# Second attention's queries projected four batches at a time, its first keys loaded earlier, and weights quantised during the first attention

## What is computed

```python
x = x + attention(layernorm(x), ctx, ctx, Wq, bq, Wk, bk, Wv, bv, Wo, bo)   # 16 heads of 16
x = x + experts(layernorm(x), classifier, bias, gate_up, down)              # router, top 6 of 40, 32 of them real experts
x = x + attention(layernorm(x), ctx, ctx, ...)                              # softmax of -0.25 * q.k
x = x + fp4_ffn(layernorm(x), w_gate, w_up, w_down)

def fp4_quant_dequant(x):            # in blocks of 16, for the weights and the activations
    scale = max(max(abs(block)) / 6, 1e-12)
    return GRID[searchsorted(MID, abs(block / scale))] * sign(block) * scale
```

## Time and profile before

| | |
|---|---|
| time, median of 3 runs (lowest, highest) | 1060.65 us (1060.6, 1065.75) |
| the profiled execution's own time | 1065.29 us |
| its span, first to last instruction | 1063.7 us |
| busy: PE, DVE, ACT, POOL | 932.7, 697.2, 414.1, 136.6 us |
| DVE row maxima (L1219), 256 | 235.5 us |
| quantising the weights on DVE, 16 batches x 9 instructions | 1.89 us more DVE time in a batch than in the first attention |
| front of the second attention, from 613.98 to the first row scores at 657.66 | PE busy 23.3 of 43.7 us, granted TensorE clock 0.79 |
| from there to the first column scores at 672.79 | PE busy 10.5 of 15.1 us, granted clock 0.73 |
| both attentions, steady part | granted clock 1.00 |

### The profile page before, as it was taken

One profiled execution on the slowest core, in us unless ns is written; L12 is line 12 of the kernel. 1 busy time (PEld: TensorE's weight loads), 2 busy tenths in 40 slices (PEclk: granted clock), 3 DMA queues, 4 the chain that ended last, 5 costly groups with the idle time before them and its releaser, 6 DMA issues.

```text
span 1063.7 us, 20769 instructions
## 1 busy us (share of the span) xinstructions
PE 932.7 (88%) x7430; PEld 724.7 (68%) x7430; DVE 697.2 (66%) x1518; ACT 414.1 (39%) x970; POOL 136.6 (13%) x129
## 2 busy tenths in 40 slices
PE   2996999999979779999998856899999987898987
PEld 1663778788857459899988745577777765455554
DVE  4454677777735715455554464788888874999995
ACT  1441566666655441111111122466565654111211
POOL 7021000000011430000000004000000001344442
PEclk9997999999986999999999978899999988999999
DMA  9688454454042630202121305554444200000000
GB/s 284 198 235 192 85 101 91 95 88 88 17 132 62 200 130 16 78 16 62 35 61 60 109 26 129 112 91 88 88 87 88 60 2 1 5 12 10 13 13 18
DMA packets 103231, 87.07 MB, mean 82 GB/s; under 512 B 44002, under 2 KB 94562, under 8 KB 103010
## 3 DMA queue, kind: packets, MB, share of 16 engines
q1 hardware_dynamic: 103122, 85.58, 33.3%
HBM read 67.52 MB, written 17.79 MB: 80 GB/s over the span
## 4 chain that ended last, share of the span: by engine, by line
issue 32%; PE 28%; DVE 27%; DMA 7%; SPq 2%; POOL 2%; ACT 1%; POOLq 0%; DVEq 0%; ACTq 0%
PE ps L794 12%; DVE ext L1219 8%; PE ps L801 7%; DMA qscr<-qsp 3%; DVE Pr L1167 2%; DVE Pr L1172 2%; DVE Pr L1170 2%; DMA Qz<-mT 2%; PE ps L651 2%; PE ps L561 2%; DMA wgu<-wgu 1%; DVE amh L1399 1%; DVE Pr L1421 1%; POOL ksp L492 1%; PE ps L700 1%
## 5 line engine op out<-in xcount | busy, mean ns | idle before, releaser
L1219 DVE TENSOR_REDUCE ext<-ps 112x2 f32<-112x750 f32 x256 | 235.5, 933 | 56.8 <-PE ps L623 54.3
L986 ACT ACTIVATE Pr<-ps 125x448 f32<-125x448 f32 x384 | 199.0, 542 | 101.9 <-PE ps L637 88.7
L794 PE MATMUL ps<-xT,wgu 128*128 128x224 f32 x704 | 150.1, 356 | 12.5 <-issue 4.9
L794 PEld LDWEIGHTS ps<-xT,wgu 128*128 128x128 f32 x704 | 132.9, 191 | 23.1 <-issue 12.4
L637 PE MATMUL ps<-Qz,Kp 98*125 98x224 f16 x768 | 132.8, 269 | 15.8 <-DMA Qz<-mT 13.7
L623 PE MATMUL ps<-Kp,Qz 96*112 96x375 f16 x512 | 123.8, 334 | 11.8 <-DMA Qz<-qscr 10.6
L637 PEld LDWEIGHTS ps<-Qz,Kp 98*125 98x125 f16 x768 | 96.4, 140 | 49.9 <-DMA Qz<-mT 18.6
L691 PE MATMUL ps<-wv,ctx 128*125 128x256 f32 x384 | 121.9, 402 | 0.8 <-ACT Vx L992 0.7
L561 PE MATMUL ps<-ctx,wk 128*128 128x375 f32 x256 | 95.1, 519 | 25.0 <-DMA bqk<-bqk 14.2
L1337 DVE TENSOR_TENSOR Pr<-Pr,ps 128x224 f32<-128x224 f32 x88 | 34.1, 388 | 125.5 <-ACT Pr L1057 68.2
L873 PE MATMUL ps<-Pr 128*112 128x352 f32 x256 | 85.5, 480 | 16.9 <-DVE Pr L1421 16.5
(11 more groups left out here) (139 smaller groups left out, 1094.9 us busy)
## 6 DMA issues: line engine op xcount, KB each, us to landing
ctx<-ctxT SPq DMA_DIRECT2D x64, 375.0 KB, 3.7
Kp<-kscr SPq DMA_DIRECT2D x96, 187.5 KB, 4.1
kscr<-ksp SPq DMA_DIRECT2D x32, 375.0 KB, 3.8
wgu<-wgu SPq DMA_DIRECT2D x32, 256.0 KB, 2.8
Qz<-qscr SPq DMA_DIRECT2D x192, 28.0 KB, 3.9
wdn<-wdn SPq DMA_DIRECT2D x32, 128.0 KB, 3.0
qscr<-qsp SPq DMA_DIRECT2D x32, 112.0 KB, 3.3
X<-x_in SPq DMA_DIRECT2D x1, 1792.0 KB, 11.7
```

The source lines that it names most:

```text
L794: last = mm(ps[:, bank, half_ * CT:(half_ + 1) * CT], wgu_sb[e % NE][:, q, EI * half_:EI * half_ + EI], xT2[:, q, c * CT:(c + 1) * CT], st ...
L986: A(Pr[g % 2][0:KC, j, GI * t:GI * t + GI, :].rearrange("r h q -> r (h q)"), ps[0:KC, 4 + k % 2, 0:GI * S], ACT.Exp, scale=scale).then_inc ...
L1219: V.tensor_reduce(ext[0:S, 2 * p:2 * p + 2], ps[0:S, 2 * (p % 2):2 * (p % 2) + 2, 0:M], AX_X, red).then_inc(row_maximum_taken, 1)
```

## The change

Four things are changed together.

1. In the second attention the queries are made in four groups of four batches. One normalise of a group fills four buffers (`xns`), eight transposes go to two banks, one copy, four projections of 448 columns, high and low parts of the group, one store of 448 KB. Statistics are computed for four batches, then for the other twelve. SP loads the queries of batch 0 when group 0 is stored, and those of batches 1 to 3 by six larger loads when group 1 is ready. The orders are strings again (`PE_FRONT`, `DVE_FRONT`), in which the row scores and maxima of batch 0 stand among the projections of groups 2 and 3, and the value projections of batch 0 behind them.
2. The keys of batches 0 to 3 and the contexts of batches 0 and 1 of the second attention are loaded in the router stage, after the last key store and before expert 4's weights. For this SP waits for all key stores.
3. The weights are quantised in the first attention. VectorE keeps three instructions per batch (block maximum, scale, reciprocal), behind the first three maxima. The scales have two buffers, and VectorE waits before writing one for the piece two before.
4. The other steps go to GpSimd: ten instructions for each piece, of another form. The power of two of each value, which VectorE took by masking bits, comes from comparisons of its square with 4 and 16. ScalarE waits for all 16 pieces before the router stage.

```diff
+PE_FRONT = "turn project turn project turn R R project R R turn R R project R R M V V V V W W"
+DVE_FRONT = "low norm norm norm low max max max max low max max max max split low copy"
+QG = 4
+NG = B // QG
-DVE_ORDER = "max max max max max max normalise max max split copy residual"
+DVE_ORDER = "max q max q max q max max max normalise max max split copy residual"
@@ SP, second attention
+                    for g in range(NG):
+                        sp.wait_ge(group_high_ready, g + 1)
+                        sp.wait_ge(group_low_ready, g + 1)
+                        sp.dma_start(qscr[QG * g:QG * (g + 1)].rearrange("b c p s m -> p (b c) (s m)"),
+                                     qsps[:, g].rearrange("p b c s q -> p (b c) (s q)")).then_inc(group_stored, 16)
+                        if g == 0:
+                            sp.wait_ge(group_stored, 16)
+                            load_queries(0, 1, first_queries_loaded)
+                        elif g == 1:
+                            load_queries(1, QG - 1, group_queries_loaded)
...
+                        if l == 1 and b == 1:
+                            sp.wait_ge(group_stored, 16 * NG)
+                        if l == 0 or b > 0:
+                            load_kq(b + 3)
@@ SP, router stage
+                    for par in (0, 1):
+                        sp.wait_ge(split_stored[par], 48 * (B // 2) + 16)
+                    sp.wait_ge(col_scores_ready, NJ * GT * B)
+                    for b in range(NR):
+                        load_keys(b)
+                    sp.wait_ge(keys_projected, 2 * B)
+                    for b in (0, 1):
+                        sp.dma_start(ctx_sb[b][:, :, :].rearrange("p c m -> p (c m)"), ctxT[b]).then_inc(
+                            values_ctx_loaded[b], 16)
@@ GpSimd, behind add_bias(0)
+            def quantise_weights(b):
...
+                pool.wait_ge(weight_scales_ready, b + 1)
+                if b > 0:
+                    pool.wait_ge(weights_quantised, b)
+                P.tensor_tensor(blocks(qrw), blocks(w0), spread(rcw[b % 2]), ALU.mult).then_inc(pool_link, 1)
+                pool.wait_ge(pool_link, 7 * b + 1)
+                P.tensor_tensor(qcw, qrw, qrw, ALU.mult).then_inc(pool_link, 1)
+                pool.wait_ge(pool_link, 7 * b + 2)
+                P.tensor_scalar(qtw, qcw, 4.0, 1.0, ALU.is_ge, ALU.add)
+                P.tensor_scalar(qcw, qcw, 16.0, 1.0, ALU.is_ge, ALU.add).then_inc(pool_link, 1)
+                pool.wait_ge(pool_link, 7 * b + 3)
+                P.tensor_tensor(qcw, qcw, qtw, ALU.mult).then_inc(pool_link, 1)
+                pool.wait_ge(pool_link, 7 * b + 4)
+                P.tensor_scalar(qrw, qrw, PRED, None, ALU.mult)
+                P.tensor_scalar(qcw, qcw, MAGIC, None, ALU.mult).then_inc(pool_link, 1)
+                pool.wait_ge(pool_link, 7 * b + 5)
+                P.tensor_tensor(qrw, qrw, qcw, ALU.add).then_inc(pool_link, 1)
+                pool.wait_ge(pool_link, 7 * b + 6)
+                P.tensor_tensor(qrw, qrw, qcw, ALU.subtract).then_inc(pool_link, 1)
+                pool.wait_ge(pool_link, 7 * b + 7)
+                P.tensor_tensor(blocks(w0), blocks(qrw), spread(scw[b % 2]), ALU.mult).then_inc(weights_quantised, 1)
@@ TensorE, front of the second attention
+                def turn_group(q):
+                    pe.wait_ge(group_normalised, QG * (q + 1))
+                    if q >= 2:
+                        pe.wait_ge(group_xT_copied, q)
...
+                def project_group(q):
+                    pe.wait_ge(group_xT_copied, q + 1)
+                    if q >= 2:
+                        pe.wait_ge(group_high_ready, q)
+                        pe.wait_ge(group_low_ready, q)
...
+                            if l == 1 and b < 0:
+                                pe.wait_ge(group_low_ready, NG)
                             project_values(g + 1, *next(values))
@@ ScalarE
+                    for q in range(NG):
+                        act.wait_ge(group_turned, q + 1)
+                        t = 4 if q else 0
+                        A(xTs[q], ps[:, t:t + 2, 0:QG * S], ACT.Copy).then_inc(group_xT_copied, 1)
+                        act.wait_ge(group_projected, q + 1)
+                        for m in range(C2):
+                            last = A(qsps[:, q, :, m, 0, :], ps[:, (6 if q else 2) + m, 0:QG * S].rearrange(
+                                "p (b q) -> p b q", q=S), ACT.Identity, bias=bqk[1][:, m:m + 1])
+                        last.then_inc(group_high_ready, 1)
...
+                    act.wait_ge(weights_quantised, B)
@@ VectorE
-            def quantise_weights(b, k):
+            def scale_weights(b, k):
+                w0 = fq[:, 16 * NW16 * b:16 * NW16 * (b + 1)]
                 if k == 0:
+                    ch.link(V.tensor_reduce(amw[:, :], w0.rearrange("p (b e) -> p b e", e=16), AX_X, ALU.max,
+                                            apply_absolute_value=True))
                 elif k == 1:
+                    if b >= 2:
+                        dve.wait_ge(weights_quantised, b - 1)
+                    ch.link(V.tensor_scalar(scw[b % 2][:, :], amw[:, :], 1.0 / 6.0, 1e-12, ALU.mult, ALU.max))
                 else:
+                    V.reciprocal(rcw[b % 2][:, :], scw[b % 2][:, :]).then_inc(weight_scales_ready, 1)
...
+                def low_group(q):
+                    dve.wait_ge(group_high_ready, q + 1)
+                    for m in range(C2):
+                        last = V.scalar_tensor_tensor(qsps[:, q, :, m, 1, :], ps[:, (6 if q else 2) + m, 0:QG * S].rearrange(
+                            "p (b q) -> p b q", q=S), bqk[1][:, m:m + 1], qsps[:, q, :, m, 0, :], ALU.add, ALU.subtract)
+                    last.then_inc(group_low_ready, 1)
...
+                elif step == "q" and l == 0:
+                    scale_weights(b, next(steps))
```

264 lines of the change are left out of this document (148 added, 116 removed).

## The result

| | before | after |
|---|---|---|
| time, median (lowest to highest), 4 runs each | 1062.12 us (1060.6 to 1065.75) | 1036.86 us (1036.01 to 1038.45) |
| ratio, 95% interval | | 0.9759 [0.9728, 0.979] |
| profiled execution, its span | 1065.29, 1063.7 us | 1036.13, 1034.4 us |

The account below looks back on a forecast made before the run. TensorE's order was taken to bound both attentions' batches, with 0.75 us more in the second for weight quantisation, and a chain its front. Terms -12.2 - 9.7 + 9.0 = -12.9 us gave 1047.8 us; 8 in 10 range 1037 to 1061.

Parts of the forecast that it names:

- Term 3: First attention: scale instructions and GpSimd collision cost 0.15 + 0.45 us in each of 15 batches, +9.0 us, bounds 0 and +25.
- part 4: First attention, VectorE: three scale instructions among the maxima delay the split, 0.15 us per batch, +2.3 us over fifteen.
- part 5: First attention: GpSimd's ten instructions keep up with the batch but hold VectorE's split, 0.45 us per batch, bounds 0 and 1.5.
- Term 2: Second attention: VectorE without the weight quantisation takes the first attention's time, -9.7 us over fourteen batches.
- The last batch: Second attention's last batch: removing the quantisation gains 0, as it stood beside waits for TensorE.
- Term 1: Second attention's front: queries four batches at once bring the copy of batch 1's maxima earlier, -12.2 us, bounds -5 and -16.
- Part 2: Router stage: loading keys and contexts there costs 0, bounds 0 and +2 us; its gain is counted in Term 1.
- No collision: Rival, first attention: the split falls in gaps or isn't held, Term 3 is 2.3 us; 1041.0 us, chance 0.22.
- Both held: Rival, first attention: GpSimd holds both halves of the split, Term 3 is 18.8 us; 1057.5 us, chance 0.17.
- front gives half: Rival, second attention's front: four-batch store, uncovered chain and low clock leave Term 1 at -5 us; 1055.0 us, chance 0.12.
- not what it says: Rival, second attention: the 0.75 us per batch isn't the quantisation's, Term 2 is 0; 1057.5 us, chance 0.03.
- Chain too long: Rival, first attention: GpSimd's chain outlasts a batch and sets its pace; 1078 us at 2.4 us per tensor_scalar, chance 0.08.

Follow-up runs that it names:

- 3: The kernel after without the three scale instructions on VectorE and GpSimd's chain, so without weight quantisation; 1036.36 us.
- 7: The kernel after with the three scale instructions moved behind the sixth maximum in VectorE's order; 1038.36 us.
- number 14: The kernel after with mostly tensor_tensors in GpSimd's chain of nearly the same length, to meet the split; weights not quantised; 1038.08 us.
- number 1: The kernel before with only the weights' move: scales on VectorE and chain on GpSimd in the first attention; 1051.57 us.
- number 2: The kernel after with the weights quantised by nine VectorE pieces in the second attention again, no GpSimd chain; 1047.67 us.
- its second trace: The kernel after, unchanged, measured again beside the front with filled idle time, on the same chip; 1034.56 us.
- numbers 3 to 7 and 14: Kernels with after's front; those without their own line: only GpSimd's last instruction kept, 1039.79 us; GpSimd's chain some 1.5 us later, 1034.91 us.
- number 10: The kernel after with group 1's normalisations ahead of low 0 and project 2 ahead of the row scores; 1028.89 us, on another chip 1029.67.
- number 9: The kernel after with the key loads of batches 0 to 3 back in the second attention's front, contexts still in the router stage; 1034.76 us.
- number 6: The kernel after with GpSimd's first multiplication done seven times, making its chain longer than a batch; 1058.86 us.
- number 8: The kernel after with group 1's normalisations ahead of low 0 in VectorE's order of the front; 1033.03 us.
- 11: Against number 10: thirteen unread matmuls behind the experts' end, and low 0 ahead of group 1's normalisations again; 1033.54 us.
- 13: Against number 10: thirteen unread matmuls on TensorE behind the experts' end, same order of the front; 1030.90 us.

## Why the prediction was wrong

**Term 3, the first attention's +9.0 us, is the step that failed.** It measured 0 within what traces scatter (173.0 to 174.2 us in after, 173.26 without the work; 173.1 and 173.2 in the means over all traces). It failed in both halves.

The links and pieces (part 4, +2.3 us of it). I took the fourth maximum 0.5 us late and carried that to the split in full, because I read "three back to back take 2.84 us" as VectorE's own rate. It was the rate of the row scores: 0.95 us each, against 0.85 that VectorE needs. The measured delay, 0.36 us, is gone by the seventh maximum. Numbers 3 and 7 show it, by taking the work away (no gain) and by putting it behind the place that makes up for it (0.21 us a batch). The sign to be read was in the earlier trace rows: 2.84 / 3 is 0.95, and a maximum in the earlier trace rows takes 0.88 to 0.94 with its overlap; engines that run back to back in one view may still be waiting in turn.

The collision (part 5, +6.8 us of it). The mechanism is there: number 14 has a hold of 0.53 us. I priced half an instruction and no slack. Measured, in after, it is 0.18 us, in ten of the sixteen batches, all within the slack of 0.37 at M, which was left whole as the links took none of it. Where the split falls in GpSimd's chain is a matter of phase, and that it met a tensor_scalar there and not a tensor_tensor was luck; number 14 prices the other case, at 0.17 us in four of the fourteen batches. The bounds 0 and +25 held the value; I chose badly between them. I had prices for both sides and gave the slack away in the step before. The duration of GpSimd's tensor_scalar was mis-sized as well: 1.19, 1.18, 0.94 and 0.93 us, where I took 0.5 within bounds of 0.4 and 1.6, and the chain takes 9.3 us from the first start to the last end, not 7.2 (bounds 6.8 to 11.6). That changed nothing, as 9.3 is under 12.2.

**Term 2, -9.7 us, was right in mechanism and too small.** Measured -12.3 us in after over the same fourteen batches, -12.0 in number 1. The undisturbed batch gave exactly the 0.75 us expected. But these two traces lie low: the fifteen with the weights moved or left out have 171.1 to 173.7 us, 172.4 in the mean, against 183.3 in the mean of before and number 2, so over these fourteen batches the term is -10.9. What else changed is what I left out: batch 0's pieces in the stretch before (2.0 us in number 1's trace, nothing measurable in after, where that stretch has another shape), what lies behind the fourteen batches, and the waits of the column scores for the flattened maxima, which vary between traces (2.1 us in before, 0.8 in after, 2.1 in its second trace). I took one pair of stretches as exact and gave this term no bounds; from the second copy to the end the same fifteen traces have 363.4 to 367.2 us, the two others 378.0 and 379.8. The difference of the means is 13.9 us. The last batch I had put at 0; what lies behind the fourteen batches is 3.0 us shorter in the means (195.6 to 192.6), but number 2, with the pieces in place, has 194.8 and the fifteen have 190.1 to 194.8, so how much of that is the pieces' stays open.

**Term 1, -12.2 us, was right.** The mean of the eight traces with the front of after (after, its second trace, numbers 3 to 7 and 14; 56.9 to 59.7) is 57.8 us, against 69.88: -12.0. Number 2, the front without the weights' move, has -11.2. Step by step, counted from the experts' end: first transposes 5.8 (measured 5.76), copy of group 0 8.6 (8.5), project 0's end 14.3 (14.3), low 0's end 16.7 (16.9), queries stored 20.8 (20.1), first row scores 26.5 (27.9), project 3's end 36 to 39 (39.9), M 41.9 (42.5), first column scores 48 to 49 (50.0). Project 1 was to be faster than project 0 and took 6.34 us, since TensorE had idled 3.93; that is the largest miss in the chain, 2 us, and number 10 gives it back.

**Part 2, 0 us,** was right twice over: nothing was pushed back (expert 4's load is issued at 408.71 us with the experts 3.4 us earlier), and number 9 shows that the front doesn't need it either.

**The rivals.** "No collision" (1041.0) is what happened, and I had given it 0.22. It is still 4 us too high, and saves 19.6 us where 25.3 were measured (before's own median moved from 1060.65 to 1062.12 with its fourth run): term 2's 4.2 and its own 2.3 us for the links account for that, with some scatter. "Both held", "front gives half" and "not what it says" fell. "Chain too long" is real as a mechanism: number 6 reaches it at 14.0 us, with +22 us. But that price is paid in two places, as VectorE's two scale buffers let GpSimd fall behind for nine batches at 1.8 us each before anyone waits.

**The range.** Its low end, 1037, took in "no collision" with 4 us to spare, and no bounds for term 2. With 363.4 to 367.2 as the scatter of one stretch alone, and 319 to 326 as that of another, a sum from one trace has some 4 us on either side before any mechanism is in doubt.

By the terms as measured, -12.0 - 13.9 + 0 = -25.9 us, against -25.3 by the medians.

## What to carry to other kernels

A delay on an engine is priced at the next place where that engine waits for someone, not where it arises: look for the maxima, copies or sums between the two that are paced from outside, and compare their spacing with what one takes at the engine's own rate. Work laid ahead of such a place is free up to what it can make up; the same work behind it costs. A collision counts only over the slack that is left there.

When a term is read off two stretches of one trace, take its bounds from what else lies in them, and say which batches the stretches don't cover. And a transfer's wait on TensorE can cost twice, by itself and by the low clock of what comes next (project 2 in number 8: 5.53 us instead of 3.25). Fill it with work that is due anyway (project 2: the second copy 3 to 5 us earlier); the matmuls that nobody reads brought nothing that the times show.

## What the runs showed of the hardware

- GpSimd, 128 x 288 float32: tensor_tensor 0.67 to 0.81 us, tensor_scalar with one operation 0.93, with two, the first a comparison, 1.18. One input isn't cheaper than two.
- A GpSimd tensor_tensor and a small VectorE tensor_scalar or scalar_tensor_tensor between SBUF tensors exclude each other, at up to 0.74 us for one of 0.17. Beside a GpSimd tensor_scalar the same ones took 0.44 us at most: held to 0.45 us behind its start when they started in its first 0.23 us, and seven times to its end when they started in its last 0.4. VectorE's reciprocal took 0.25 to 0.27 us in all seven traces, with a GpSimd instruction beside it or without.
- TensorE ran the same eight matmuls in 3.24 to 3.27 us (granted clock 1.00) or in 4.7 to 6.3 us. The slow ones of the front came behind idle stretches of 3.33, 3.55, 3.93, 4.51 and 6.85 us, each with four row scores or eight transposes in between. The length of the idle stretch just before doesn't settle it: behind 1.88 or 1.89 us project 2 took 3.25 us in numbers 10, 11 and 13, and 4.94 in number 10's second trace.
